# Attention scores from split fp32r operands, a pipeline one step deeper, and one buffer of shifted halves

## The chip, the cores and the metric

The program runs on one core of a Trainium2 chip. The metric is the device time of that core in microseconds, lower is better. Engines are named as the profile names them: PE is TensorE (PEld its weight loads), DVE is VectorE, ACT is ScalarE, POOL is GpSimd, SP issues most DMAs.

## The reference, cut to what matters

A first stage mixes three attentions (compressed, selected, windowed) into `x` of shape (2, 2048, 256), followed by layer norms. The change leaves it alone. Then come two layers of this form, everything in float32:

```python
h = shift_token(x)                     # second half of the channels comes from the token before
q, k, v = split(h @ wqkv)              # 8 heads of 64, 512 columns each
q = l2norm(q) * qs;  k = l2norm(k) * ksc
q, k = rotary_xpos(q, k)
sim = einsum('bhwid,bhwjd->bhwij', bq * 8, look_around(bk))    # 128 queries, 256 keys
o = softmax(where(mask, -big, sim)) @ look_around(bv)
x = x + o @ wo
h = layernorm(shift_token(x)) @ w1 + b1
a, g = split(h)
x = x + (a * gelu(g)) @ w2 + b2
```

The 4096 tokens are 32 blocks of 128. A block of queries sees its own keys and those of the block before.

## The kernel before, in words

One layer is an attention phase over 32 blocks (64 in the two layers) and a feed-forward phase over 8 groups of four blocks. The phases are separated by `end_phase`, at which all engines meet.

**Attention phase.** Each engine has its own function `step(n, i)`, a list of calls in an order fixed by hand. In step n an engine works on several blocks at once, each at another stage: `live(n, lag)` guards a call for block n − lag. The first steps are written out, the middle is a loop of two steps, and the last are written out again. Semaphore waits stand in the called helpers; those under `if type(b) is int` are only in the written-out steps. The calls for one block:

- POOL `stage_h` copies the block and its shifted half (`hs_attn`) to `h_in`. PE `transposes` turns it (L1662). ACT `hi` rounds it to fp32r (`hT_hi`), DVE `lo` subtracts to get the low part `hT_lo` (L2304).
- PE `project(b, 0|1|2)` makes q, k, v in banks 0, 1, 2 as three fp32r products (L1698 to L1700): high by high, high by low, low by high.
- ACT `square` (L1102), DVE `sums` (L2351) with a floor of 1e-24 (L2355), and POOL `root` with the power −1/2 (L771) give the inverse norms. DVE `sines` (L2333) and `cosines` (L2318) multiply the raw q or k by the rotary tables, POOL `add_up` (L785) adds them, DVE `normalise_k` (L2363) scales k.
- PE `turn_qk` transposes q and k (L1722), ACT `q_out` and `k_out` copy them to `qT` and `kT`, which are plain float32.
- PE `scores(b, part)` makes the scores of four heads a part (L1770). A head has 64 channels, so two heads at a time lie in the two halves of the array's rows, and their results go to banks 3 and 4:

```python
for j in (2 * part, 2 * part + 1):
    for e in range(2):
        rows64 = slice(e * DH, (e + 1) * DH)
        mm = pe.matmul(bank[:, 3 + e, ...], qT[rows64, j], kT[rows64, j]..., start=True, stop=True)
```

- DVE `hide` masks a head and takes its maximum (L2436), ACT `exponent` takes the exponential and its sum (L1180), DVE `inverses` inverts two sums and waits for the result (L2465). `weigh` scales a head's probabilities: five heads on DVE (L2471), two on ACT (L1189), one on POOL (L791).
- PE `turn_probs` transposes two heads (L1824), ACT `probs_out` copies them out (L1211), PE `values` multiplies by v (L1856), ACT `values_out` copies that to `oT`, PE `project_out` multiplies by `wo` into bank 5 (L1783), DVE `add_rows` adds to `x_sb` (L2476). `turn_probs(b, 1)` writes bank 5 too, so it waits for `add_rows`. ACT `v_out` copies v to `v_sb` (L1136), into the half that `values` of the block before last has just read, and `project(b, 2)` of the next block waits for it.

**Feed-forward phase.** PE `up` (L1921 to L1923) and `down` (L1936 to L1938) multiply by w1 and w2 as three fp32r products each; `down` has 128 x 256 results. While group g is worked on, the normalised input of the next group is made: DVE `norm_stats`, ACT `norm_apply` (L1283), PE `turn_norm` (L1904), ACT `norm_hi` (L1272), DVE `norm_full` (L2544), POOL `norm_lo` (L826). The last group of a layer does this too, for group 0 again, and nobody uses it. In the second layer ACT also makes the final norm of the group before (`last_norm`, L1293).

**Shifted halves.** SP moves the second half of every block down by one token, to `hs_attn` for the attention phase and to `hs_ffn` for the feed-forward phase.

Of the kernel before, what the change touches and what calls it, by code (L numbers as in the profile page):

```python
# [7 lines left out]
ALU = mybir.AluOpType  # L8
# [5 lines left out]
P = 128  # L14
# [20 lines left out]
MADE = 24  # L35
# [30 lines left out]
def build(nc, x0, Wq, bq, Wk, bk, Wv, bv, Wo, bo, Wg, bg, Wc, bc, Ws, bs,  # L66
          wqkv, q_scale, k_scale, wo, ln_g, ln_b, w1, b1, w2, b2, rope_base, out):
    with ExitStack() as ctx:
# [15 lines left out]
        hs_attn = place("hs_attn", [P, NB + B, P])  # L84
        hs_ffn = place("hs_ffn", [P, NB + B, P])
# [36 lines left out]
        qT = place("qT", [P, HEADS // 2, P])  # L122
        kT = place("kT", [P, HEADS // 2, 2, P])
# [109 lines left out]
        assert base[0] <= hs_at + 8 * (NB + B) * P  # L233
# [9 lines left out]
        HIDDEN = (0, 1, 2, 3, 6, 7, 4, 5)  # L243
        EXPED = (0, 1, 2, 3, 6, 4, 7, 5)
        INVERTED = (0, 1, 3, 2)
        TURNED = (0, 1, 3, 2)
        P_OUT = (0, 1, 3, 2)
        VALUED = (1, 0, 3, 2)
        P_DVE = (1, 0, 2, 4, 6)
        P_ACT = (7, 5)  # L250
        P_POOL = (3,)
# [12 lines left out]

        def later(b, n):

            return min(b + n, NB - 1) if type(b) is int else b + n

        def sin_operand(lay):

            return pT[:] if lay else hs_ffn[:, 1:9, :].rearrange("p (a s) n -> p a (s n)", a=2)
# [116 lines left out]
        qT_ready = sem("qT_ready")  # L388
        v_ready = sem("v_ready")
# [13 lines left out]
        hs_ffn_moved = sem("hs_ffn_moved")  # L403
# [18 lines left out]
        hs_attn_moved = sem("hs_attn_moved")  # L422
# [33 lines left out]
        def _(sp):  # L456
# [68 lines left out]
            def move_group(g):  # L525

                sp.wait_ge(x_made, GB * (g + 1))
                shift_down(hs_attn, g * GB + g // GPB, x_sb[:, g * GB:(g + 1) * GB, P:D], GB, hs_moved)
# [18 lines left out]
            for lay in range(DEPTH):  # L547
# [16 lines left out]
                for first, last in ((0, GB), (GB, NB)):  # L564
                    with sp.Fori(first, last) as t:

                        sp.wait_ge(x_attn, 1 + lay * NB + t + 1)
                        shift_down(hs_ffn, t + t // BPB, x_sb[:, bass.ds(t, 1), P:D], 1, hs_ffn_moved)
                    if first == 0:
                        sp.wait_ge(hs_ffn_moved, 48 * (NB * lay + GB))  # L570
                        settle(sp)
                sp.wait_ge(hs_ffn_moved, 48 * NB * (lay + 1))
# [6 lines left out]
                if lay + 1 < DEPTH:  # L579
# [33 lines left out]
        def _(pool):  # L613
# [54 lines left out]
            pool.wait_ge(sc_made, MADE - 2)  # L668
# [4 lines left out]
            pool.memset(hs_attn[:], 0.0).then_inc(sc_made, 1)  # L673
            pool.memset(hs_ffn[:], 0.0).then_inc(sc_made, 1)
# [57 lines left out]
            for lay in range(DEPTH):  # L732
# [19 lines left out]
                def stage_h(b):  # L752

                    if type(b) is int:
                        if follows(b, 1):
                            pool.wait_ge(hT_ps, k0 + b)
                    settle(pool)
                    pool.tensor_copy(h_in[:, 0], x_sb[:, b, 0:P]).then_inc(h_staged, 1)
                    pool.tensor_copy(h_in[:, 1], hs_attn[:, b + b // BPB, :]).then_inc(h_staged, 1)

                def root(b, which, part):

                    if which == 1:
                        pool.wait_ge(ss_floor[1], k0 + b + 1)
# [3 lines left out]
                    elif which == 0:  # L768
                        pool.wait_ge(ss_floor[0], k0 + b + 1)
# [17 lines left out]
                def weigh(b, h):  # L787

                    pool.wait_ge(inverted, nth(INVERTED, k0 + b, 1))
# [9 lines left out]
                def step(n, i):  # L799
                    if i == 0 and live(n, 4) and live(n, 2):  # L800
# [5 lines left out]
                    if live(n, 0):  # L806
                        stage_h(n)
                    if live(n, 1):
                        add_up(n - 1, 0)
                        root(n - 1, 1, 2)  # L810
                        add_up(n - 1, 1)
# [16 lines left out]
                n0 = lay * (NG + 1)  # L828
# [32 lines left out]
                def group(u, i, first, before):  # L861
# [7 lines left out]
                    norm_scales(n0 + g + 1)  # L869
                    if before:  # L870
                        last_root(g - 1, 1 - i)
                    norm_lo(n0 + g + 1, 1 - i)
# [6 lines left out]
                with pool.Fori(0, NG // 2 - 1) as u:  # L879
                    for i in range(2):  # L880
                        group(u + 1, i, False, last)
                if not last:
# [1813 lines left out]
```

## Time and profile before

| | |
|---|---|
| median of 3 runs | 1615.21 us (1614.42 to 1616.76) |
| the profiled execution, its own time | 1614.17 us |
| its span, first to last instruction | 1612.4 us |
| first stage, up to the first attention phase | 270.5 us |
| attention phase, layer 0 and layer 1 (first L1662 to first L1904) | 445 us and 444 us |
| granted TensorE clock, mean | 0.971 |

Times in the rows are microseconds from the first instruction, unless marked ns. A matmul's time in a row runs to the end of its result, so matmuls that follow each other overlap in the records; the distance between starts is what each one costs PE. A float32 matmul stands as two MATMUL records of half the work, an fp32r matmul and a transpose as one.

### The profile page before, as it was taken

How to read it: one execution, taken by the hardware profiler on the slowest of the kernel's cores; microseconds unless marked ns; L12 is line 12 of the kernel's file. 1: busy time of each engine (PE TensorE's matmuls, PEld its weight loads, DVE VectorE, ACT ScalarE, POOL GpSimd, SP SyncE). 2: the span in 40 equal slices, each digit the busy share in tenths (PEclk: the TensorE clock that was granted, in tenths of full speed). 3: DMA queues.
4: the chain of work that ended last, by engine and by line, in shares of the span. 5: the costliest groups of instructions: out<-in, count | busy, mean ns of one | idle time of the engine just before them, and what ended most of it. 6: DMA issues, size and time to landing. Idle time of an engine off the chain costs nothing.

```text
span 1612.4 us, 34824 instructions
## 1 busy us (share of the span) xinstructions
PE 1505.1 (93%) x9859; PEld 1204.0 (75%) x9859; DVE 1165.4 (72%) x3485; ACT 1009.4 (63%) x2564; POOL 704.5 (44%) x782
## 2 busy tenths in 40 slices
PE   8899992999999999979999959999999999799996
PEld 6467871688787888858888837878787887688885
DVE  6762785888888888875656568888888888666664
ACT  5123574677777777755454538777777778345553
POOL 4013255555555555532222255555555554244442
PEclk9999996999999999999999979999999999899998
DMA  5003134000000000002000020000000000000101
GB/s 174 1 1 110 50 113 126 4 6 6 5 5 5 5 5 5 5 8 87 8 14 7 13 63 5 6 5 5 5 5 5 5 5 7 30 27 27 52 26 52
DMA packets 57513, 43.92 MB, mean 27 GB/s; under 512 B 13214, under 2 KB 55386, under 8 KB 57442
## 3 DMA queue, kind: packets, MB, share of 16 engines
q1 hardware_dynamic: 57442, 43.07, 8.8%
q8 instruction: 33, 0.54, 0.1%
q14 instruction: 38, 0.31, 0.1%
HBM read 26.24 MB, written 8.39 MB: 21 GB/s over the span
## 4 chain that ended last, share of the span: by engine, by line
PE 77%; DVE 9%; ACT 5%; issue 4%; POOL 2%; DVEq 1%; ACTq 1%; DMA 0%; POOLq 0%; SPq 0%; PEldq 0%
PE bank L1770 8%; PE bank L1856 8%; PE bank L1783 7%; PE bank L1824 7%; PE bank L1698 6%; PE bank L1699 5%; PE bank L1700 5%; PE bank L1722 4%; PE bank L1921 3%; PE bank L1922 3%; PE bank L1923 3%; PE bank L1582 2%; PE bank L1936 2%; PE bank L1938 2%; PE bank L1937 2%
## 5 line engine op out<-in xcount | busy, mean ns | idle before, releaser
L771 POOL TENSOR_TENSOR rnorm<-sumsq,neg_half 128x8 f32<-128x8 f32 x128 | 211.0, 1649 | 204.2 <-DVE sumsq L2355 204.2
L1180 ACT ACTIVATE prob<-prob,neg_max 128x256 f32<-128x256 f32 x512 | 253.4, 500 | 1.5 <-DVE neg_max L2436 1.5
L785 POOL TENSOR_TENSOR qk_cos<-qk_cos,qk_sin 128x512 f32<-128x512 f32 x128 | 163.6, 1278 | 132.7 <-DVE qk_cos L2318 131.9
L1698 PE MATMUL bank<-wqkv_hi,hT_hi 128*128 128x512 f32 x384 | 176.9, 461 | 2.9 <-DVE hT_lo L2304 1.9
L1700 PE MATMUL bank<-wqkv_hi,hT_lo 128*128 128x512 f32 x384 | 154.0, 401 | 0.0
L1699 PE MATMUL bank<-wqkv_lo,hT_hi 128*128 128x512 f32 x384 | 153.9, 401 | 0.0
L1921 PE MATMUL bank<-h_hi,w_hi 128*128 128x512 f32 (+1 forms) x352 | 143.2, 407 | 10.3 <-POOL h_lo L826 10.3
L1312 ACT ACTIVATE act_hi<-act_full 128x512 fp32r<-128x512 f32 x96 | 60.9, 634 | 140.5 <-DVE act_full L2622 140.5
L1770 PE MATMUL bank<-kT,qT 64*128 64x256 f32 x1024 | 146.1, 404 | 2.0 <-DVE neg_max L2436 2.0
L1211 ACT ACTIVATE pT<-bank 128x512 f32<-128x512 f32 x256 | 144.5, 591 | 1.9 <-PE bank L1856 1.8
L1923 PE MATMUL bank<-h_lo,w_hi 128*128 128x512 f32 (+1 forms) x352 | 140.9, 400 | 0.0
L1922 PE MATMUL bank<-h_hi,w_lo 128*128 128x512 f32 (+1 forms) x352 | 140.9, 400 | 0.0
L1856 PE MATMUL bank<-pT,v_sb 128*64 128x128 f32 x2048 | 140.2, 279 | 0.5 <-ACT pT L1211 0.5
L2627 DVE TENSOR_TENSOR act_lo<-act_full,act_hi 128x512 fp32r<-128x512 f32 x96 | 87.6, 913 | 69.2 <-ACT act_hi L1312 69.2
L2471 DVE TENSOR_SCALAR prob<-prob,pinv 128x256 f32<-128x256 f32 x320 | 116.0, 396 | 28.8 <-DVE pinv L2465 3.9
L1824 PE MATMUL bank<-ident,prob 128*128 128x128 f32 x1024 | 133.6, 273 | 2.8 <-ACT prob L1189 2.6
L1856 PEld LDWEIGHTS bank<-pT,v_sb 128*64 128x64 f32 x2048 | 109.1, 136 | 32.3 <-ACT pT L1211 21.5
L2622 DVE SCALAR_TENSOR_TENSOR act_full<-bank,b_sb,gelu_sb 128x512 f32<-128x512 f32 x96 | 71.9, 749 | 84.3 <-ACT gelu_sb L1308 60.1
L1783 PE MATMUL bank<-wo_sb,oT 128*128 128x256 f32 x512 | 124.0, 386 | 8.1 <-issue 8.1
L1824 PEld LDWEIGHTS bank<-ident,prob 128*128 128x128 f32 x1024 | 117.4, 141 | 13.3 <-DVE prob L2471 4.1
L1770 PEld LDWEIGHTS bank<-kT,qT 64*128 64x128 f32 x1024 | 88.8, 187 | 42.5 <-issue 33.1
L2333 DVE TENSOR_TENSOR qk_sin<-bank,rope 128x512 f32<-128x512 f32 x128 | 88.6, 692 | 40.8 <-ACT qk_sq L1102 40.8
(270 smaller groups left out, 3721.2 us busy)
## 6 DMA issues: line engine op xcount, KB each, us to landing
x_sb<-in_L_attn_hidden_states SPq DMA_DIRECT2D x8, 512.0 KB, 7.1
x_in<-in_L_attn_hidden_states SPq DMA_DIRECT2D x8, 512.0 KB, 4.5
x_scratch<-x_in SPq DMA_DIRECT2D x8, 512.0 KB, 3.0
f_x<-x_scratch SPq DMA_DIRECT2D x8, 512.0 KB, 4.1
out<-f_y SPq DMA_DIRECT2D x8, 512.0 KB, 3.0
raw<-in_L_ffn_w SPq DMA_DIRECT2D x6, 640.0 KB
hs_attn<-x_sb SPq DMA_DIRECT2D x16, 224.0 KB
hs_ffn<-x_sb SPq DMA_DIRECT2D x64, 56.0 KB, 2.0
```

The costliest lines, as they stand in the source:

```text
L771: pool.tensor_tensor(rnorm[:, part * HEADS:(part + 1) * HEADS], sumsq[:, which * HEADS:(which + 1) * HEADS], neg_half[:, 0:HEADS], ALU.pow ...
L1180: act.activation(prob[:, h], prob[:, h], ACT.Exp, bias=neg_max[:, h:h + 1], scale=-1.0, accum_out=psums[:, h:h + 1]).then_inc(exped, 1)
L1698: pe.matmul(bank[:, to], hT_hi[:, c], wqkv_hi[:, c, cols], start=(c == 0), stop=False)
L1699: pe.matmul(bank[:, to], hT_hi[:, c], wqkv_lo[:, c, cols], start=False, stop=False)
L1700: mm = pe.matmul(bank[:, to], hT_lo[:, c], wqkv_hi[:, c, cols], start=False, stop=(c == DC - 1))
L1770: mm = pe.matmul(bank[:, 3 + e, (j % 2) * 2 * P:(j % 2 + 1) * 2 * P], qT[rows64, j], kT[rows64, j].rearrange("p a b -> p (a b)"), start=Tr ...
L1783: mm = pe.matmul(bank[:, 5, 0:D], oT[:, c], wo_sb[:, c], start=(c == 0), stop=(c == INNER // P - 1))
L1824: tr = pe.transpose(bank[:, 6 - j % 2, ((h % 2) * 2 + c) * P:((h % 2) * 2 + c + 1) * P], prob[:, h, c], ident[:])
L1856: mm = pe.matmul(bank[e * DH:(e + 1) * DH, 7, j * P:(j + 1) * P], v_sb[:, c, h * DH:(h + 1) * DH], pT[:, j % 2, (e * 2 + c) * P:(e * 2 + c ...
L1921: pe.matmul(to, w1_hi[:, c, cols], h_hi[:, half, c], start=(c == 0), stop=False)
L1922: pe.matmul(to, w1_lo[:, c, cols], h_hi[:, half, c], start=False, stop=False)
L1923: mm = pe.matmul(to, w1_hi[:, c, cols], h_lo[:, half, c], start=False, stop=(c == DC - 1))
```

## The change

Four things change.

- `qT` and `kT` become fp32r, `qT_lo` and `kT_lo` are new. DVE makes them (`q_lo`, `k_lo`) by subtracting the rounded values from banks 0 and 1. `scores` makes three products, q by k, q by k_lo, q_lo by k.
- Of DVE's five heads, head 1 is now scaled by ACT and head 4 by POOL; the floor of 1e-24 moves from DVE to POOL (`root`).
- Every engine's step is put in another order with another set of lags; the output projection is five blocks behind instead of four. Eight steps ahead of the loop and five behind it are written out, instead of six and four.
- `hs_attn` and `hs_ffn` become one buffer `hs`. The last group of a feed-forward phase no longer makes a next input, and the last two groups are written out behind the loop. POOL clears one buffer less, ACT clears `kT_lo` once a layer more.

```diff
-        qT = place("qT", [P, HEADS // 2, P])
-        kT = place("kT", [P, HEADS // 2, 2, P])
+        qT = place("qT", [P, HEADS // 2, P], F32R)
+        kT = place("kT", [P, HEADS // 2, 2, P], F32R)
-        P_DVE = (1, 0, 2, 4, 6)
-        P_ACT = (7, 5)
-        P_POOL = (3,)
+        P_DVE = (0, 2, 6)
+        P_ACT = (1, 7, 5)
+        P_POOL = (3, 4)
...
                     for j in (2 * part, 2 * part + 1):
-                        for e in range(2):
-                            rows64 = slice(e * DH, (e + 1) * DH)
-                            mm = pe.matmul(bank[:, 3 + e, (j % 2) * 2 * P:(j % 2 + 1) * 2 * P], qT[rows64, j],
-                                           kT[rows64, j].rearrange("p a b -> p (a b)"), start=True, stop=True)
+                        for n, (q, k) in enumerate(((qT, kT), (qT, kT_lo), (qT_lo, kT))):
+                            for e in range(2):
+                                rows64 = slice(e * DH, (e + 1) * DH)
+                                mm = pe.matmul(bank[:, 3 + e, (j % 2) * 2 * P:(j % 2 + 1) * 2 * P], q[rows64, j],
+                                               k[rows64, j].rearrange("p a b -> p (a b)"), start=(n == 0), stop=(n == 2))
...
+                def q_lo(b):
+                    dve.wait_ge(qT_ready, k0 + b + 1)
...
+                    dve.tensor_tensor(qT_lo[:], bank[:, 0].rearrange("p (c t) -> p c t", t=P), qT[:], ALU.subtract).then_inc(qT_lo_ready, 1)
+                def k_lo(b, half):
+                    dve.wait_ge(kT_ready, k0 + b + 1)
...
+                    dve.tensor_tensor(kT_lo[:, :, half], bank[:, 1].rearrange("p (c t) -> p c t", t=P), kT[:, :, half], ALU.subtract).then_inc(kT_lo_ready, 1)
...
-                    dve.tensor_scalar(sumsq[:, part], sumsq[:, part], 1e-24, None, ALU.max).then_inc(ss_floor[which], 1)
+                    pool.tensor_scalar(some, some, 1e-24, None, ALU.max).then_inc(ss_floor[which], 1)
+                    pool.wait_ge(ss_floor[which], k0 + b + 1)
...
-                        if j == 3:
+                        if j == 3 and more(u * 2 + i):
                             turn_norm(n + 1)
```

The order of a step on PE, in the loop, before: `project_out` (n − 4), v of n − 1, the input transposes of n, k turned, the probabilities of n − 2, then q of n:

```order
L1783 MATMUL bank<-wo_sb,oT 128x256 x4
L1698 MATMUL bank<-wqkv_hi,hT_hi 128x512
...
L1662 MATMUL bank<-ident,h_in 128x128 x2
L1722 MATMUL bank<-ident,qk_cos 128x128 x4
L1824 MATMUL bank<-ident,prob 128x128 x4
...
L1770 MATMUL bank<-kT,qT 128x256 x4
```

and after the change (the products are L1730 to L1732, scores L1811, probabilities turned L1865, values L1897, q and k turned L1758):

```order
L1824 MATMUL bank<-wo_sb,oT 128x256 x4
L1730 MATMUL bank<-wqkv_hi,hT_hi 128x512
...
L1865 MATMUL bank<-ident,prob 128x128 x4
...
L1811 MATMUL bank<-kT,qT 128x256 x2
L1811 MATMUL bank<-kT_lo,qT 128x256 x2
L1811 MATMUL bank<-kT,qT_lo 128x256 x2
...
L1897 MATMUL bank<-pT,v_sb 64x128 x4
L1758 MATMUL bank<-ident,qk_cos 128x128 x4
```

Four float32 matmuls of a part became twelve fp32r ones (the three rows shown stand twice in a part); k of n − 1 is now projected first, both parts stand behind a projection or the values, and k and q are turned together near the end of the step.

On DVE, around `add_rows` (writes `x_sb`) and `lo` (writes `hT_lo`) in the loop, the order before is

```order
L2363 TENSOR_TENSOR qk_cos<-qk_cos,rnorm 128x512
...
L2465 RECIPROCAL pinv<-psums 128x2
...
L2471 TENSOR_SCALAR prob<-prob,pinv 128x256 x2
...
L2476 TENSOR_TENSOR x_sb<-bank,x_sb 128x256
...
L2304 TENSOR_TENSOR hT_lo<-bank,hT_hi 128x256
L2351 TENSOR_REDUCE sumsq<-qk_sq 128x8
L2355 TENSOR_SCALAR sumsq<-sumsq 128x8
```

and after the change, over the end of a step and the beginning of the next,

```order
L2413 TENSOR_TENSOR kT_lo<-bank,kT 128x4x128
...
L2527 RECIPROCAL pinv<-psums 128x2
...
L2345 TENSOR_TENSOR hT_lo<-bank,hT_hi 128x256
L2533 TENSOR_SCALAR prob<-prob,pinv 128x256 x2
...
L2527 RECIPROCAL pinv<-psums 128x2
...
L2403 TENSOR_TENSOR qT_lo<-bank,qT 128x512
...
L2538 TENSOR_TENSOR x_sb<-bank,x_sb 128x256
```

Before, `add_rows` (there L2476) stood ahead of `hT_lo` (L2304) of the same step, and nothing of the kind of `kT_lo` and `qT_lo` existed; now `add_rows` comes behind `hT_lo`, two scaled heads, a reciprocal and `qT_lo` of the step before.

## Rows read from the trace of the kernel before

**Rows 1.** The page's busy times of the engines over the whole span.

```profile
PE 1505.1 (93%) x9859; PEld 1204.0 (75%) x9859; DVE 1165.4 (72%) x3485; ACT 1009.4 (63%) x2564; POOL 704.5 (44%) x782
```

**Rows 2.** Busy times in one step of the attention loop; the first row names the columns.

```profile
core 0: us, PE busy (x) PEld busy (x) DVE busy (x) ACT busy (x) POOL busy (x), PEclk, DMA share, GB/s
410.72:424.00 13.28, 13.28 (x101) 10.64 (x101) 10.80 (x37) 10.38 (x30) 7.07 (x9) 1.00 0.02 5
```

**Rows 3.** The chain that ended last, same step: start, us, what.

```profile
410.72 1.73 PE bank L1783 x8
412.68 0.23 PE bank L1699
...
419.43 0.87 PE bank L1824 x8
420.30 1.02 PE bank L1856 x16
421.32 1.06 PE bank L1770 x8
...
424.00 1.73 PE bank L1783 x8
```

**Rows 4.** Timeline of one score part: start, us, engine, line; two, then eight matmuls.

```profile
403.42 0.49 PE L1770 MATMUL bank<-kT,qT 64*128 64x256 f32 x2
403.42 0.73 PEld L1770 LDWEIGHTS bank<-kT,qT 64*128 64x128 f32 x8 [0.36 <-issue]
403.42 1.13 PE L1770 MATMUL bank<-kT,qT 64*128 64x256 f32 x8
```

**Rows 5.** Timeline of PE in the feed-forward phase, ends of twelve matmuls of `down`.

```profile
819.31 0.28 PE L1936 MATMUL bank<-w_hi,act_hi 128*128 128x256 f32 x1
...
820.73 0.39 PE L1921 MATMUL bank<-h_hi,w_hi 128*106 128x512 f32 x1
```

**Rows 6.** Groups of DVE, 400 to 500 us: busy us, mean ns, idle before.

```profile
L2471 DVE TENSOR_SCALAR prob<-prob,pinv 128x256 f32<-128x256 f32 x38 | 13.9, 399 | 3.3 <-DVE pinv L2465 0.2
L2333 DVE TENSOR_TENSOR qk_sin<-bank,rope 128x512 f32<-128x512 f32 x15 | 10.4, 692 | 4.2 <-ACT qk_sq L1102 4.2
...
L2465 DVE RECIPROCAL pinv<-psums 128x2 f32<-128x2 f32 x30 | 4.8, 161 | 1.7 <-DVE pinv L2465 1.7
L2304 DVE TENSOR_TENSOR hT_lo<-bank,hT_hi 128x256 fp32r<-128x256 f32 x8 | 3.4, 425 | 6.5 <-ACT hT_hi L1089 6.5
L2476 DVE TENSOR_TENSOR x_sb<-bank,x_sb 128x256 f32 x8 | 3.2, 405 | 0.0
L2355 DVE TENSOR_SCALAR sumsq<-sumsq 128x8 f32<-128x8 f32 x15 | 2.6, 172 | 2.6 <-DVE sumsq L2351 0.8
```

**Rows 7.** Groups of ACT and POOL in the same stretch.

```profile
L1136 ACT ACTIVATE v_sb<-bank 128x512 f32<-128x512 f32 x7 | 4.2, 598 | 3.3 <-PE bank L1856 3.3
...
L771 POOL TENSOR_TENSOR rnorm<-sumsq,neg_half 128x8 f32<-128x8 f32 x15 | 24.7, 1648 | 25.9 <-DVE sumsq L2355 25.9
...
L791 POOL TENSOR_SCALAR prob<-prob,pinv 128x256 f32<-128x256 f32 x8 | 5.1, 640 | 7.5 <-DVE pinv L2465 7.5
```

**Rows 8.** The chain through the first steps of layer 0.

```profile
270.53 0.68 PE bank L1662 x2
...
277.63 0.61 ACT qk_sq L1102
...
283.13 0.66 PE bank L1722 x4
...
285.83 2.03 PE bank L1770 x8
```

**Rows 9.** Feed-forward phases: layer 0 and end of layer 1, two chain rows, one timeline row.

```profile
814.39 0.87 PE bank L1904 x8
...
1592.71 1.57 ACT f_y L1293 x3
...
1597.50 0.38 PE L1936 MATMUL bank<-w_hi,act_hi 42*128 42x256 f32 x1 [2.17 <-DVE act_lo L2627]
```

More of the change, by code:

```diff
@@ L83, in build @@
         hs_at = base[0]
[L84 to L85 removed]
+        hs = place("hs", [P, NB + B, P])
+        qT_lo = place("qT_lo", [P, HEADS // 2, P], F32R)
+        kT_lo = place("kT_lo", [P, HEADS // 2, 2, P], F32R)
+        sin_0 = place("sin_0", [P, 2, BPB * 32])
+        place("spare", [P, 10 * P])
         ident = place("ident", [P, P])
@@ L263, in follows, with more @@
             return type(b) is not int or b >= n
+        def more(g):
+            return type(g) is not int or g + 1 < NG
         def later(b, n):
@@ L878, in _ @@
                 group(0, 1, False, last)
-                with pool.Fori(0, NG // 2 - 1) as u:
+                with pool.Fori(0, NG // 2 - 2) as u:
                     for i in range(2):
                         group(u + 1, i, False, last)
+                for i in range(2):
+                    group(NG // 2 - 1, i, False, last)
                 if not last:
@@ L1072, in _ @@
                 act.wait_ge(x1_stored, 16 * NG)
-                act.activation(kT[:, :, 1], zero[:, 0:1, None].broadcast_to([P, HEADS // 2, P]), ACT.Copy).then_inc(kv_zero, 1)
+                for k in (kT, kT_lo):
+                    act.activation(k[:, :, 1], zero[:, 0:1, None].broadcast_to([P, HEADS // 2, P]), ACT.Copy).then_inc(kv_zero, 1)
                 act.activation(v_sb[:, 1], zero[:].broadcast_to([P, INNER]), ACT.Copy).then_inc(kv_zero, 1)
@@ L1264, in _ @@
                         step(u * 2 + i, i)
-                for n in range(NB, NB + 3):
+                for n in range(NB, NB + 4):
                     step(n, n % 2)
@@ L1327, in _ @@
                 group(0, 1, False, last)
-                with act.Fori(0, NG // 2 - 1) as u:
+                with act.Fori(0, NG // 2 - 2) as u:
                     for i in range(2):
                         group(u + 1, i, False, last)
+                for i in range(2):
+                    group(NG // 2 - 1, i, False, last)
                 if not last:
@@ L1962, in _ @@
                     group(0, i, i == 0)
-                with pe.Fori(0, NG // 2 - 1) as u:
+                with pe.Fori(0, NG // 2 - 2) as u:
                     for i in range(2):
                         group(u + 1, i, False)
+                for i in range(2):
+                    group(NG // 2 - 1, i, False)
                 for j in range(FC - 2, FC):
@@ L2636, in group @@
                             last_moments(g - 1, 1 - i)
-                        if j == 3:
+                        if j == 3 and more(g):
                             norm_full(n)
@@ L2647, in _ @@
                 group(0, 1, False, last)
-                with dve.Fori(0, NG // 2 - 1) as u:
+                with dve.Fori(0, NG // 2 - 2) as u:
                     for i in range(2):
                         group(u + 1, i, False, last)
+                for i in range(2):
+                    group(NG // 2 - 1, i, False, last)
                 add_up(lay * NG + NG - 1, NG - 1)
```

411 lines of the change are left out of this document (223 added, 188 removed).

## The prediction

> **What bounds the kernel now.** I read the busy times first: PE is busy in 93% of the span, the next engine, DVE, in 72% [rows 1]. An average hides stages, so I then cut one step out of the attention loop [rows 2]: PE is busy in all of its 13.28 us at the full granted clock, while DVE has 10.80 us of work, ACT 10.38 and POOL 7.07. The chain of waits says the same in another way [rows 3]: from one output projection (410.72) to the next (424.00) every piece is a piece of PE, and it waits for nobody. The loop therefore costs what PE's matmuls cost. DVE has 2.5 us of room in a step, ACT 2.9, POOL 6.2. The 64 blocks at 13.28 us would be 850 us of the 1614, so a change of 0.1 us a step moves the total by 6.4 us.
>
> What PE pays for: a 512-column fp32r matmul 0.23 us, eight transposes 0.87, sixteen value matmuls 1.02, the output projection 1.73, and a score part 1.06, twice a step [rows 3].
>
> **The score parts, the term that carries the sum.** A part before is four float32 matmuls, eight records. The first two together end after 0.49 us, all eight after 1.13 [rows 4], so the three later pairs follow at (1.13 − 0.49) / 3 = 0.213 us. The two heads of a pair thus run at once, in the two halves of the rows: eight in a row at 0.213 would be 1.70 us, and the part takes 1.06. Of these 1.06, 4 x 0.213 = 0.85 is streaming, and 0.21 is the first weight load and the switch into and out of half arrays.
>
> A part now is six pairs of fp32r matmuls of 256 columns. No row shows an fp32r pair in half arrays. The nearest row is `down`, fp32r with 256 columns over the full array: twelve of them take 820.73 − 819.31 = 1.42 us, 0.118 each, and every one has its own weights, so their loads are hidden [rows 5]. I take 0.118 for a pair, since the float32 pair shows that a second head costs nothing [rows 4]. The part becomes 0.21 + 6 x 0.118 = 0.92 us, 0.14 less. The number of switches between full and half arrays in a step stays six. Over 128 parts: **−17.9 us**. Bounds: half of the float32 pair's 0.213 is 0.107, which would save another 0.07 a part, 8 us in all; no overlap of the two heads is the other end, a rival below.
>
> One rule speaks against taking 0.118. The rows of the float32 part show that loads run under matmuls of the same half: eight loads end 0.73 us after the start, the matmuls 1.13 [rows 4]. The Trainium skill (TensorE: Matmul & The Clock Gate, Part 3 on packing small matmuls) says that a weight load overlaps matmuls in flight only if its row group differs, though Part 2 of the page also allows it for a load into the background buffer. By the sentence of Part 3 the total would be the second rival's, 1666 us; the trace sides with Part 2.
>
> **DVE.** New: `qT_lo` and `kT_lo`, each 128 x 512 from PSUM. Of that form is the sine product, 692 ns [rows 6]; twice is +1.38 us a step. Gone: two floors, 2 x 0.172, and two of five scaled heads, 2 x 0.399. DVE goes from 10.80 to about 11.04 us, plus some 0.2 us behind each reciprocal, in a step of 13.0. It is covered by PE with nearly 2 us left, so the work itself costs nothing; if PE's cover went, all of 0.24 us a step would show.
>
> **ACT and POOL.** ACT gets one head, 0.5 us: 10.9 in 13.0. POOL gets one head, 0.64 [rows 7], and two floors, each under the 0.64 of that much larger operation and perhaps 0.3: 7.07 becomes 8.3. Costs nothing. A floor now stands ahead of the power of 1.65 us [rows 7] and lengthens the way to `rnorm` by about 0.2 us, but its readers, the masks, come a step later.
>
> **The order.** What decides is whether a wait ends late. I laid the step out, PE from the start of `project_out`: k 1.73 to 3.13, four heads turned to 4.0, scores to 5.0, q to 6.5, turned to 7.4, values to 8.4, scores to 9.4, values to 10.5, k and q turned to 11.4, v to 12.8, input transposes to 13.0. Then I put the others behind it. The tight places:
> - `turn_probs(1)` waits for `add_rows`. After the input transposes DVE has `hT_hi` by ACT (about 0.4 and 0.2 to get there), `hT_lo` 0.43, two heads 0.80, a reciprocal with its wait 0.38, `qT_lo` 0.69, `add_rows` 0.41 [rows 6]: 3.3 us. PE meanwhile has 1.73 + 6 x 0.23 + 0.44 = 3.57 [rows 3]. Slack 0.25.
> - `project` of v waits for `v_out`, which waits for the last values: 0.60 [rows 7] and 0.3 of handing over, against eight transposes and a switch, about 1.0. Slack 0.1 to 0.2.
> - The second score part waits for four masks: 2.4 us after the first part, against 3.3 us of PE work. Slack 0.9. k turned waits for POOL's sum and `normalise_k`: slack 0.6 or more. Input transposes wait for the last mask: 0.7.
>
> All are positive, so the loop stays PE's, at 13.28 − 0.28 = **13.00 us**. SP's moves come one step later and are not waited for in the loop. Since two slacks are small, I charge 0.02 us a step, +1.2 us.
>
> **Filling and draining.** Before, the first score part begins 15.3 us after the first transposes and itself takes 2.03 us, twice its time in the loop; v of block 0 lies under the way from the squares (277.63) to the turned k (283.13) [rows 8]. Now v stands behind the turned k and q, so that way is bare, and `qT_lo` is added: I make it 16.9 us. The second part waits 0.8 us longer for masks, and k of block 2 waits for `hT_lo`; against that come the cheaper parts, already counted. About +2.4 us. At the drain one more step stands, but the same work lies behind the last scores: 0 to −0.5. Bounds +0.5 and +5 a layer; I take 2, for two layers **+4 us**.
>
> **The feed-forward phases.** Turning the unused input goes: 0.87 us of PE [rows 9] in each layer. At the very end PE stands 2.17 us before the last `down`: ACT's final norm (from 1592.71) and the unused norms before it delay the last activation [rows 9]. ACT and DVE lose more than PE there; I give the second layer 1.6. Together **−2.5 us**. The two groups written out are the same instructions: 0. The merged buffer: slot t is overwritten five steps after it was read, no wait: 0. POOL's cleared buffer lies in a wait, ACT's extra one beside POOL's rotary tables: 0.
>
> **Sum.** −17.9 + 1.2 + 4 − 2.5 = −15.2 us. Against the profiled execution's own 1614.17 this is 1599; its median counterpart is 1615.21, 1.0 above, so **1600.0 us**. A measurement of this kernel can tell about 0.2% from no change, 3.2 us.
>
> **Rivals.**
> 1. *Small waits eat the gain.* If `v_out` or `add_rows` is late by 0.1 to 0.24 us a step, 64 steps give back 6 to 15 us: 1606 to 1615. For: slacks of 0.1 to 0.25 are as small as my errors of handing over. Against: DVE and ACT have 2 us of room. 13%.
> 2. *Loads are bare.* If each pair first waits for its weights, by half of the 0.21 beside the streaming, a pair costs 0.118 + 0.105: the part becomes 6 x 0.223 + 0.105 = 1.44, 0.38 more than now, 128 of them +49, total 1666. The trace of float32 speaks against it [rows 4]. 4%.
> 3. *The two heads of an fp32r pair run one after the other* (the other side, slower). Place: PE's score parts. Twelve times 0.118 plus 0.21 is 1.63, +0.57 a part, +73 us, total 1691. It decides from a pair of 0.136 us up: from there the parts give back the whole 15 us. For: fp32r streams a column in 0.46 ns, faster than a float32 record, and no row shows two such streams. Against: two heads of 64 rows read no more than one full array does [rows 5]. 5%.
> 4. *The DVE chain becomes a bound*, above 0.24 us late a step: slower than before, 1618 to 1635. 4%.
> 5. *Better than forecast*: pairs at 0.107, or filling free: 1586 to 1594. 7%.
>
> **Numbers.** The forecast, 1595 to 1606, has 67%. The range 1591 to 1616 adds nearly all of rival 1 and half of 5, about 83%. Faster: 67 + 7 + 8 of rival 1's 13, 0.82. Within 0.2%: the other 5, 0.05. Slower: 4 + 5 + 4, 0.13.
>
> **What would show it.** In the changed trace a score part should last 0.92 us on the chain, with 12 records, and six pairs 0.12 apart; the output projections should lie 13.00 us apart, and PE should have no idle time but in the first three steps of a layer. DVE should be busy 11.0 to 11.3 us a step. PE waits on `x_sb` or `v_sb` in the loop would be rival 1; starts of a pair 0.12 apart instead of 0.01 rival 3; 0.22 between pairs rival 2. A step above 13.28 makes the forecast wrong, and so does a fill above 20 us.

## The result, and the profile after

| | before | after |
|---|---|---|
| median | 1614.42 us (1613.72 to 1616.76, 5 runs) | 1606.59 us (1605.55 to 1607.81, 5 runs) |
| span of the profiled execution | 1612.4 us | 1604.8 us |

The ratio is 0.9948, interval 0.9934 to 0.9963: faster by 0.5%, 8 us. The forecast was 15 us. The busy times of the page, against [rows 1]:

```profile
PE 1488.4 (93%) x10355; PEld 1218.0 (76%) x10355; DVE 1175.1 (73%) x3329; ACT 1025.1 (64%) x2610; POOL 771.9 (48%) x961
```

Two steps of the loop, cut from one output projection to the next, against [rows 2], with the same columns:

```profile
413.95:427.05 13.10, 13.10 (x111) 10.95 (x110) 11.11 (x35) 10.71 (x31) 8.45 (x11) 1.00 0.02 5
427.05:440.06 13.01, 13.01 (x111) 10.79 (x109) 11.22 (x35) 10.79 (x31) 8.26 (x10) 1.00 0.02 5
```

PE is still busy in all of both, at the full granted clock. A step is 13.10 and 13.00 us in turn, 13.05 on average, where it was 13.28. Where that comes from stands in PE's timeline of one score part, between the turned probabilities and the projection of q (start, us, engine, line, what), against [rows 4]:

```profile
418.12 0.39 PE L1811 MATMUL bank<-kT,qT 64*128 64x256 f32 x2
418.34 0.28 PE L1811 MATMUL bank<-kT_lo,qT 64*128 64x256 f32 x2
418.46 0.28 PE L1811 MATMUL bank<-kT,qT_lo 64*128 64x256 f32 x2
418.57 0.28 PE L1811 MATMUL bank<-kT,qT 64*128 64x256 f32 x2
418.69 0.29 PE L1811 MATMUL bank<-kT_lo,qT 64*128 64x256 f32 x2
418.81 0.29 PE L1811 MATMUL bank<-kT,qT_lo 64*128 64x256 f32 x2
419.03 0.50 PE L1730 MATMUL bank<-wqkv_hi,hT_hi 128*128 128x512 f32 x1
```

Six pairs: the second to the sixth start 0.11 to 0.12 us apart, the first and the last take 0.22 each, with the switch into and out of half arrays. That makes 419.03 − 418.12 = 0.91 us for the part. It was 1.06.

So the loop gains nearly what was forecast, and more than half of that is gone elsewhere. I cut both traces at the same places: the first input transposes of a layer, the second score part of block 2, that of block 31, the first turned norm. The fill is the stretch of first steps in which the pipeline is not yet full, the drain the one of last steps.

| us | before, layers 0 and 1 | after | forecast a layer |
|---|---|---|---|
| up to the first attention phase | 270.5 | 270.0 | 0 |
| to the second part of block 2 (the fill) | 44.5, 42.9 | 48.5, 49.1: **+4.0, +6.3** | +2, less 0.7 for five cheaper parts |
| from there to block 31, 29 steps | 382.4, 382.3 | 376.0, 376.0: **−6.4, −6.3** | −7.5 |
| from there to the turned norm | 18.3, 19.3 | 18.9, 18.9 | −0.1 to −0.6 |
| feed-forward phase | 223.3, 228.9 | 220.9, 226.6: **−2.4, −2.4** | −0.9, −1.6 |

The fill is the surprise. PE's timeline there, layer 0, first of the kernel before and then of the changed one; the bracket is PE's idle time and who ended it:

```profile
278.53 0.66 PE L1722 MATMUL bank<-ident,qk_cos 128*128 128x128 f32 x4 [0.94 <-POOL qk_cos L785]
278.95 0.48 PE L1698 MATMUL bank<-wqkv_hi,hT_hi 128*128 128x512 f32 x1
...
280.43 0.38 PE L1662 MATMUL bank<-ident,h_in 128*128 128x128 f32 x2
283.13 0.66 PE L1722 MATMUL bank<-ident,qk_cos 128*128 128x128 f32 x4 [2.32 <-DVE qk_cos L2363]
```

```profile
276.34 0.40 PE L1732 MATMUL bank<-wqkv_hi,hT_lo 128*128 128x512 f32 x1
281.17 1.97 PE L1758 MATMUL bank<-ident,qk_cos 128*128 128x128 f32 x8 [4.43 <-DVE qk_cos L2421]
282.79 0.78 PE L1730 MATMUL bank<-wqkv_hi,hT_hi 128*128 128x512 f32 x1
...
285.50 0.63 PE L1690 MATMUL bank<-ident,h_in 128*128 128x128 f32 x2
287.06 0.50 PE L1730 MATMUL bank<-wqkv_hi,hT_hi 128*128 128x512 f32 x1 [0.93 <-DVE hT_lo L2345]
...
292.95 0.39 PE L1811 MATMUL bank<-kT,qT 64*128 64x256 f32 x2 [1.72 <-DVE neg_max L2494]
294.75 0.66 PE L1758 MATMUL bank<-ident,qk_cos 128*128 128x128 f32 x4 [0.82 <-DVE qk_cos L2421]
295.88 0.66 PE L1758 MATMUL bank<-ident,qk_cos 128*128 128x128 f32 x4 [0.46 <-POOL qk_cos L798]
...
299.08 0.50 PE L1730 MATMUL bank<-wqkv_hi,hT_hi 128*128 128x512 f32 x1 [0.93 <-DVE hT_lo L2345]
...
311.55 0.50 PE L1730 MATMUL bank<-wqkv_hi,hT_hi 128*128 128x512 f32 x1 [0.93 <-DVE hT_lo L2345]
```

Before, q is turned at once, and the 1.5 us of v and the input transposes of block 1 (278.95 to 280.8) lie under the wait for the turned k. After the change the way from the squares through POOL's power to the turned k is bare: 4.43 us. Behind it the same work comes late and at half clock: v's six matmuls start 0.43 us apart instead of 0.23 (282.79 to 285.50, 2.7 us with the first load, for 1.5), and then the next block's `hT_lo` is bare too.

The waits add up as follows. At the first turned q and k PE idles 4.43 us, where it idled 0.94 + 2.32 before: 1.2 more. The masks ahead of the second score part cost 1.72 for 1.00, the turned k and q of block 1 0.82 + 0.46 for none. And PE waits 0.93 us for `hT_lo` three times more, 2.8 us, the largest piece; waits of 0.41 and 0.54 us for `v_sb` and a mask are gone. That is some 5 us more idle time, of which the cheaper score parts leave the 4.0 of the table. No wait here is ended by SP's moves or by POOL's fourth head. The floor on POOL adds 0.12 us to a way: from the end of the sums to the start of the power it is 0.62 us (275.83 to 276.45) and was 0.50 (278.95 to 279.45).

Busy times and granted clock of the same three stretches of layer 1, before and after:

```profile
939.05:954.20 15.15, 10.96 (x42) 7.74 (x44) 5.55 (x11) 3.64 (x7) 5.89 (x6) 0.76 0.56 148
954.20:969.20 15.00, 12.90 (x77) 8.78 (x74) 13.53 (x46) 10.10 (x31) 8.56 (x11) 1.00 0.00 1
969.20:982.00 12.80, 12.69 (x110) 9.84 (x107) 11.31 (x38) 11.25 (x33) 7.83 (x9) 1.00 0.01 3
```

```profile
934.86:950.00 15.14, 9.73 (x29) 7.31 (x28) 6.62 (x9) 3.08 (x6) 5.06 (x7) 0.66 0.58 148
950.00:965.00 15.00, 10.48 (x57) 7.80 (x58) 10.67 (x33) 7.75 (x24) 8.36 (x13) 0.89 0.01 2
965.00:984.00 19.00, 18.07 (x163) 14.68 (x163) 16.63 (x50) 15.56 (x42) 13.76 (x17) 1.00 0.01 1
```

PE is idle 42.95 − 36.55 = 6.4 us before and 49.14 − 38.28 = 10.9 after: 4.5 of the 6.2 us (42.95 to 49.14) are idle time. In the other 1.7 PE does the same work as before but for the score parts, which are cheaper, so what is left is the lower clock (0.66 and 0.89 granted, for 0.76 and 1.00).

### The profile page after: what moved, and what is told of

The parts are those of the page before. It is cut to its first block, busy times and chain, and to the rows that moved or that the text cites. A ratio compares the mean times of both kernels' runs of the same rounds, so it can differ in the third digit from the quotient of the medians.

```text
span 1604.8 us, 35975 instructions
## 1 busy us (share of the span) xinstructions
PE 1488.4 (93%) x10355; PEld 1218.0 (76%) x10355; DVE 1175.1 (73%) x3329; ACT 1025.1 (64%) x2610; POOL 771.9 (48%) x961
## 4 chain that ended last, share of the span: by engine, by line
PE 80%; DVE 8%; ACT 4%; issue 3%; POOL 2%; DVEq 1%; DMA 0%; ACTq 0%; POOLq 0%; SPq 0%; PEldq 0%
PE bank L1897 8%; PE bank L1811 7%; PE bank L1865 7%; PE bank L1824 7%; PE bank L1730 6%; PE bank L1732 6%; PE bank L1731 6%; PE bank L1758 4%; PE bank L1960 4%; PE bank L1961 4%; PE bank L1962 4%; PE bank L1975 2%; PE bank L1610 2%; PE bank L1977 2%; PE bank L1976 2%
## 5 line engine op out<-in xcount | busy, mean ns | idle before, releaser
L798 POOL TENSOR_TENSOR qk_cos<-qk_cos,qk_sin 128x512 f32<-128x512 f32 x128 | 180.5, 1411 | 50.9 <-DVE qk_cos L2359 48.9
L1730 PE MATMUL bank<-wqkv_hi,hT_hi 128*128 128x512 f32 x384 | 178.5, 465 | 7.5 <-DVE hT_lo L2345 7.5
L1126 ACT ACTIVATE qk_sq<-bank 128x512 f32<-128x512 f32 x128 | 76.9, 601 | 133.8 <-PE bank L1732 133.8
L1732 PE MATMUL bank<-wqkv_hi,hT_lo 128*128 128x512 f32 x384 | 154.6, 403 | 0.0
L1897 PE MATMUL bank<-pT,v_sb 128*64 128x128 f32 x2048 | 140.2, 279 | 0.5 <-ACT pT L1237 0.5
L1237 ACT ACTIVATE pT<-bank 128x512 f32<-128x512 f32 x256 | 137.9, 592 | 1.7 <-PE bank L1897 1.7
L1865 PE MATMUL bank<-ident,prob 128*128 128x128 f32 x1024 | 133.4, 273 | 3.5 <-DVE prob L2533 2.4
L1865 PEld LDWEIGHTS bank<-ident,prob 128*128 128x128 f32 x1024 | 118.9, 141 | 22.8 <-DVE prob L2533 3.5
L2494 DVE CUSTOM_DVE_ANT_0 prob<-bank,mask_odd,rnorm 128x256 f32<-128x256 f32 x256 | 115.4, 480 | 24.1 <-PE bank L1811 13.2
L2494 DVE CUSTOM_DVE_ANT_0 prob<-bank,mask_even,rnorm 128x256 f32<-128x256 f32 x256 | 115.7, 480 | 18.5 <-DVE pinv L2527 7.2
L1897 PEld LDWEIGHTS bank<-pT,v_sb 128*64 128x64 f32 x2048 | 109.1, 136 | 20.4 <-issue 10.3
L2392 DVE TENSOR_REDUCE sumsq<-qk_sq 128x8 f32<-128x512 f32 x128 | 87.4, 683 | 36.5 <-ACT qk_sq L1126 36.2
```

The lines of the kernel that those rows point to most:

```text
L1730: pe.matmul(bank[:, to], hT_hi[:, c], wqkv_hi[:, c, cols], start=(c == 0), stop=False)
L1732: mm = pe.matmul(bank[:, to], hT_lo[:, c], wqkv_hi[:, c, cols], start=False, stop=(c == DC - 1))
L1865: tr = pe.transpose(bank[:, 6 - j % 2, ((h % 2) * 2 + c) * P:((h % 2) * 2 + c + 1) * P], prob[:, h, c], ident[:])
L1897: mm = pe.matmul(bank[e * DH:(e + 1) * DH, 7, j * P:(j + 1) * P], v_sb[:, c, h * DH:(h + 1) * DH], pT[:, j % 2, (e * 2 + c) * P:(e * 2 + c ...
L2494: dve.tensor_tensor_reduce(prob[:, h].rearrange("p a b -> p (a b)"), bank[:, 3 + h % 2, (h // 2 % 2) * 2 * P:(h // 2 % 2 + 1) * 2 * P], ma ...
```

## The experiments

My theory after this result: the products save 19 us or so, the unused norm 2.5 to 4, and the new order gives back about 10 in the fill and adds nothing in the loop. The rival: the new order and the lighter DVE are what makes room for the low parts, and the fill is the price. A smaller question was why every second step takes 0.1 us more. All ratios are against the kernel before, run beside it.

### The products back to float32

```diff
-        qT = place("qT", [P, HEADS // 2, P], F32R)
-        kT = place("kT", [P, HEADS // 2, 2, P], F32R)
+        qT = place("qT", [P, HEADS // 2, P])
+        kT = place("kT", [P, HEADS // 2, 2, P])
...
-                        for n, (q, k) in enumerate(((qT, kT), (qT, kT_lo), (qT_lo, kT))):
+                        for n, (q, k) in enumerate(((qT, kT),)):
```

> The changed kernel with the old products: qT and kT are float32 again and a part is four float32 matmuls; DVE still makes qT_lo and kT_lo, which nobody reads. Theory A (the split products carry the gain): a part goes from 0.91 back to 1.06 us, a step from 13.05 to 13.35, 128 parts give 19 us, total about 1625, slower than the kernel before by 10, since the fill of the new order stays. Rival B (the new order and the lighter DVE carry the gain, the products only part of it): under 1615.

Measured: 1625.33 us, ratio 1.0072 (1.0058 to 1.0086). Steps of 13.40 and 13.29, PE busy in all of one:

```profile
418.00:431.40 13.40, 13.40 (x102) 10.81 (x101) 11.08 (x35) 10.70 (x30) 8.51 (x11) 1.00 0.02 5
```

The products alone are worth 1.0072 − 0.9948, 1.2% or 20 us, more than the whole change brings. All the rest together costs 11 us: in this run's trace the fills are 9.7 us longer than before and the two times 29 steps 4.9, against 3.6 less in the feed-forward phases. So with the same float32 products a step of the new order is not free either: 13.40 and 13.29 us in turn for 13.28.

### The kernel before without the unused norm

```diff
-                        if j == 3:
+                        if j == 3 and more(u * 2 + i):
                             turn_norm(n + 1)
```

and the same guard at the other engines' calls, with the last two groups written out.

> The kernel before with only the last group's unused norm left out and the last two groups written out. In the trace of the changed kernel the two feed-forward phases are 2.4 and 2.35 us shorter, where 0.87 and 1.6 were forecast. Theory A: all of that is this part, total 4.7 us less, 1609.7. Rival B: it is the 0.87 of PE and the last activations alone, 2.5 us less, 1612, and the rest comes from elsewhere (the merged buffer).

Measured: 1610.90 us, ratio 0.9979 (0.9970 to 0.9988), −3.4 us, between the two theories. From the first matmul of `up` to the last of `down` a layer takes 1.1 and 2.0 us less than before; in the changed kernel it takes 1.5 and 2.5 less, and what the 0.5 a layer come from stays open. The other 0.9 that the feed-forward phase of the changed kernel gains in layer 0 is the way from the first turned norm to the first `up`, which takes 6.2 to 7.1 us in different executions: scatter.

### An earlier start in the fill of the changed kernel

```diff
+                    if type(n) is int and n == 1:
+                        project(n - 1, 2, v_raw)
+                        transposes(n)
+                        turn_qk(n - 1, 1)
+                        turn_qk(n - 1, 0)
+                        return
```

on PE, with `hi(1)` and `lo(1)` moved ahead on ACT and DVE.

> The changed kernel; in step 1 of a layer alone, v of block 0 and the input transposes of block 1 stand ahead of the turned k and q on PE, and hT of block 1 is made earlier by ACT and DVE. Theory A (the new order lays bare the way from the squares to the turned k, PE idles 4.4 us and its clock halves for the next 6.8): PE idles 2 us or less there, the first score part begins about 15 us after the first transposes instead of 18.7, 3.5 to 4 us less a layer, total 1599. Rival B (the fill is bound by the chain through DVE and POOL in step 2, root of q behind stage_h): 1 us less a layer or nothing, 1605 to 1607.

Measured: 1602.75 us, ratio 0.9932 (0.9918 to 0.9945), about 2.6 us less than the changed kernel by the ratios, 3.2 in the two fills of the traces. The first score part comes 16.4 and 16.9 us after the first transposes instead of 18.7 and 17.9, but of these 2.3 and 1.1 us layer 0 keeps only 0.7 to the second part of block 2, while layer 1 gains 2.4. The result lies between the two theories. The place was right, the size not: v now lies in the wait, but what is left of it still stands, another wait appears behind the turned q, and the clock is half again just behind them.

```profile
280.88 1.09 PE L1760 MATMUL bank<-ident,qk_cos 128*128 128x128 f32 x8 [2.96 <-DVE qk_cos L2429]
283.20 0.76 PE L1732 MATMUL bank<-wqkv_hi,hT_hi 128*128 128x512 f32 x1 [1.24 <-DVE kT_lo L2421]
```

### PE's loop of four steps

```diff
-                with pe.Fori(4, NB // 2) as u:
-                    for i in range(2):
-                        step(u * 2 + i, i)
+                with pe.Fori(2, NB // 4) as u:
+                    for i in range(4):
+                        step(u * 4 + i, i % 2)
```

> The changed kernel with four steps instead of two in PE's loop. In its trace steps last 12.99 and 13.10 us by turns, and the longer one has 0.10 more in the output projection, the first work behind the loop's jump. Theory A (the jump bares the first weight load): three steps of four last 12.99, half of 24 jumps a layer less at 0.10, 1.2 to 2.5 us less, total 1604.5 to 1605.5. Rival B (another wait of even and odd steps, as POOL's mask copy): steps still alternate, no change.

Measured: 1604.40 us, ratio 0.9945 (0.9932 to 0.9959). Steps of 12.99, 12.99, 13.09, 12.99: the 0.1 us belongs to the jump of PE's loop, since the other engines' loops were left as they are. Right behind it stands `project_out`, whose 1.54 us become 1.64. It is worth 0.7 us a layer in the trace, too little for the medians.

### The old order with the split products

```diff
+                        pe.wait_ge(lo_ready, 2 * (k0 + b) + 2)
...
                     if live(n, 1):
+                        q_lo(n - 1)
                         normalise_k(n - 1)
...
                         sums(n - 1, 0)
+                        k_lo(n - 1, 1 - i)
```

`lo_ready` counts both low parts; the products are those of the change; the buffers of the low parts lie where `w2_lo` does, which is written only later.

> The kernel before, in its old order, with the three fp32r products and the two subtractions alone (q_lo ahead of normalise_k, k_lo behind the sums of q's squares; all five heads stay on DVE). Theory A, the order and the lighter DVE are needed to harvest the cheap products: by the rows of before, qT_lo fits, but kT_lo can end at 416.6 where the scores begin at 416.70, everything behind it on DVE is 0.6 us later, and the second score part then finds its fourth mask about 0.2 to 0.3 us late; DVE has 12.2 us of work a step. Steps of 13.1 to 13.35 us, total 1606 to 1616 with a DVE-released PE wait ahead of the second part, and a shorter fill than the changed kernel's (q still a step ahead). Theory B, the order is not needed: steps of 12.98 us, total 1595 to 1600, better than the changed kernel, because its fill stays that of before plus about 1 us.

Measured: 1608.68 us, ratio 0.9966 (0.9953 to 0.9979). Steps of 12.98 and 13.35 in layer 0, 12.98 and 13.15 in layer 1: the total is in theory A's range, the average step (13.17 and 13.07 us) at the lower end of its steps, and the wait is at another place than it had. It is not the fourth mask but `add_rows`, in `turn_probs(1)`:

```profile
426.12 0.41 DVE L2507 TENSOR_TENSOR x_sb<-bank,x_sb 128x256 f32 x1
```

```profile
426.75 0.65 PE L1835 MATMUL bank<-ident,prob 128*128 128x128 f32 x4 [0.19 <-DVE x_sb L2507]
```

and DVE is idle for 0.3 us in the 5.7 ahead of that row, both times behind a reciprocal. The fill is much nearer to that of before, 44.9 and 44.8 us for 44.5 and 42.9.

### The changed kernel with one product

```diff
-                        for n, (q, k) in enumerate(((qT, kT), (qT, kT_lo), (qT_lo, kT))):
+                        for n, (q, k) in enumerate(((qT, kT),)):
```

> The changed kernel with only the first of the three products (q by k in fp32r); the two low parts are still made, nobody reads them, so the scores are less exact. Theory A, PE is the bound and nothing stands close behind: four pairs of 0.116 us go from each part, a part becomes 0.45 us, a step 13.05 - 0.93 = 12.12 us, total 1606 - 60 = 1547 us. Theory B, the chain of DVE and ACT is close behind PE (11.1 us of work on DVE and some 0.2 us behind each reciprocal): steps of 12.3 to 12.7 us with PE waiting for x_sb, v_sb or masks, total 1558 to 1585 us.

Measured: 1583.82 us, ratio 0.9815 (0.9801 to 0.9829); steps of 12.55 and 12.72, not 12.12. Of the 0.93 us taken from a step only 0.41 come through. The next bound is close behind PE, as theory B said, but it is at the turned q and not at `x_sb`, `v_sb` or a mask:

```profile
417.13 0.60 ACT L1126 ACTIVATE qk_sq<-bank 128x512 f32<-128x512 f32 x1 [1.51 <-PE bank L1732]
...
421.18 0.68 DVE L2374 TENSOR_TENSOR qk_sin<-bank,rope 128x512 f32<-128x512 f32 x1
...
421.78 0.68 DVE L2359 TENSOR_TENSOR qk_cos<-bank,rope 128x512 f32<-128x512 f32 x1
...
422.64 1.56 POOL L798 TENSOR_TENSOR qk_cos<-qk_cos,qk_sin 128x512 f32<-128x512 f32 x1 [0.66 <-DVE qk_cos L2359]
...
424.44 0.63 PE L1758 MATMUL bank<-ident,qk_cos 128*128 128x128 f32 x4 [0.50 <-POOL qk_cos L798]
```

That way goes from the projected k over ACT's squares to DVE, through the sums, products and masks that DVE has in its order ahead of q's two products, and over POOL's addition. POOL's power (419.07 to 420.74) is not on it. Its slack in the changed kernel is thus about 0.4 us, and not the 0.25 at `add_rows` that I had as the smallest.

### Heads 1 and 4 back on DVE

```diff
-        P_DVE = (0, 2, 6)
-        P_ACT = (1, 7, 5)
-        P_POOL = (3, 4)
+        P_DVE = (0, 1, 2, 6, 4)
+        P_ACT = (7, 5)
+        P_POOL = (3,)
```

> The changed kernel with heads 1 and 4 scaled on DVE again, as before. DVE gets 0.8 us more a step, 11.9 in 13.05. Theory A, the slack that I forecast for add_rows ahead of the second turning of probabilities (0.25 us) is right: head 1 stands in that chain with 0.4 us, PE waits 0.15 us a step for x_sb, total 1614 to 1617 us. Theory B, the slack is 0.4 us or more and the rebalancing is worth nothing in this order: steps of 13.05 us, total 1605 to 1608 us.

Measured: 1610.06 us, ratio 0.9977 (0.9968 to 0.9986). Neither theory's number: 3.5 us more than the changed kernel by the medians, 4.7 by the ratios. In the trace the step grows in layer 0 alone, to 13.18 in the steps with the jump (1.8 us over the layer), and again at the turned k and q, 1.00 us instead of 0.87:

```profile
425.24 1.24 PE L1755 MATMUL bank<-ident,qk_cos 128*128 128x128 f32 x8
426.24 0.48 PE L1727 MATMUL bank<-wqkv_hi,hT_hi 128*128 128x512 f32 x1
```

No wait for `x_sb` appears, so that slack was 0.4 us or more. The remaining 1.7 to 2.9 us I can't place in the trace; they stay open.

### POOL's sum of q behind the scaled k

```diff
                     elif which == 0:
...
+                            if b == 0:
+                                pool.wait_ge(qk_ready[1], k0 + 1)
```

> The changed kernel with one wait more: POOL's sum of q of block 0 waits for DVE's normalise_k of block 0, in each layer's fill. Theory A, the 1.73 us of that normalise_k (0.68 in the loop) come from DVE and POOL working on SBUF at the same time: it takes 0.70 us, k is turned 1.0 us earlier, q about 0.5 later than k, the first score part begins 18.1 us after the first transposes instead of 18.7; total 1 us less, 1605 to 1606. Theory B, the 1.73 has another cause (the first use, the low clock of the fill): it stays 1.7, POOL's sum begins only behind it, the fill becomes 0.8 to 1.0 us longer a layer, total 1608.

Measured: 1606.90 us, ratio 0.9956 (0.9942 to 0.9970). In the changed kernel, DVE's `normalise_k` of block 0 and POOL's two additions:

```profile
279.38 1.73 DVE L2421 TENSOR_TENSOR qk_cos<-qk_cos,rnorm 128x512 f32<-128x512 f32 x1 [0.69 <-POOL qk_cos L798]
```

```profile
278.09 2.48 POOL L798 TENSOR_TENSOR qk_cos<-qk_cos,qk_sin 128x512 f32<-128x512 f32 x2
```

and with the added wait:

```profile
279.85 0.69 DVE L2423 TENSOR_TENSOR qk_cos<-qk_cos,rnorm 128x512 f32<-128x512 f32 x1 [0.54 <-POOL qk_cos L800]
```

```profile
280.81 1.26 POOL L800 TENSOR_TENSOR qk_cos<-qk_cos,qk_sin 128x512 f32<-128x512 f32 x1 [1.00 <-DVE qk_cos L2423]
```

The cause is theory A's: the two operations were in each other's way. The gain is not: the first score part comes 19.6 and 18.0 us after the first transposes, no earlier. PE's timeline with the added wait, layer 0:

```profile
282.13 1.12 PE L1760 MATMUL bank<-ident,qk_cos 128*128 128x128 f32 x4 [0.42 <-POOL qk_cos L800]
...
287.16 0.79 PE L1732 MATMUL bank<-wqkv_hi,hT_hi 128*128 128x512 f32 x1 [0.93 <-DVE hT_lo L2347]
...
290.02 0.58 PE L1813 MATMUL bank<-kT,qT 64*128 64x256 f32 x2
```

Counted from the first transposes (269.96 in the changed kernel, 270.42 here), k is turned 1.0 us earlier, q 0.4 and v begins 0.35 earlier. Behind that the clock takes it back: the six matmuls from the wait for `hT_lo` to the first score part last 290.02 − 287.16 = 2.86 us at half clock, where the changed kernel has them at full clock in 288.66 − 287.06 = 1.60. In layer 1 v and the input transposes behind it run at half clock for longer, and the 0.35 us are gone by `hT_lo`. So a shorter wait in the fill was worth only what the granted clock left of it.

### Both fills and the loop together

```diff
-                    if live(n, 1):
+                    if type(n) is int and n == 2:
+                        project(n - 1, 2, v_raw)
+                        turn_qk(n - 1, 1)
+                        turn_qk(n - 1, 0)
+                    elif live(n, 1):
```

on top of the early start and the loop of four, with `v_out(0)` a step earlier on ACT.

> The changed kernel with three edits together: the early start of e3_fill (v of block 0 and the input transposes of block 1 ahead of the first turned k), the same for v of block 1 one step later, and PE's loop of four steps instead of two. Theory A, the fill and the jump are what the changed kernel leaves on the table, and they add up: 1602.8 of e3_fill, minus 2 times 0.7 for the jumps, minus 2 times 0.5 for v under the second wait for the turned k: 1600 to 1601 us. Theory B, the fill's waits only move to the next late thing: 1602 to 1604 us.

Measured: 1602.69 us, ratio 0.9923 (0.9909 to 0.9937). The trace shows the attention phases at 440.5 and 439.2 us, 2.2 less each than with the early start alone, more than theory A's 1.2; the medians show nothing over it (1602.75). By the medians it is theory B's range, and the difference is inside the scatter: inconclusive.

### The old order with one head less on DVE

```diff
-        P_DVE = (1, 0, 2, 4, 6)
-        P_ACT = (7, 5)
+        P_DVE = (0, 2, 4, 6)
+        P_ACT = (1, 7, 5)
...
                         exponent(n - 1, 3)
+                        weigh(n - 1, 1)
```

on top of the old order with the split products and of the left-out unused norm.

> The order of the kernel before, with the fp32r products and subtractions of e5_before_split, head 1 scaled by ACT instead of DVE, and the last group's unused norm left out. In e5_before_split PE waited in every second step, 0.41 us in layer 0 and 0.20 in layer 1, for x_sb, with DVE never idle there. Theory A, DVE was only overfull: with one head off DVE (0.4 us a step) every step is 12.98 us, 30 times 0.18 and 30 times 0.08 us go, and with 3 us of the unused norm the total is 1597 to 1599 us; the new order is not needed, and it costs its longer fill. Theory B, the old order cannot hold the two low parts ahead of its scores whatever DVE's load (kT_lo ends 0.3 us behind the scores' turn): a wait of 0.2 us or more a step stays, now ahead of the scores, total 1604 to 1610 us.

Measured: **1596.60 us** (1594.81 to 1598.83), ratio 0.9882 (0.9867 to 0.9898): 18 us faster than before and 10 faster than the changed kernel. A step, with every engine's busy time:

```profile
409.50:422.50 13.00, 13.00 (x111) 10.82 (x110) 11.76 (x38) 10.71 (x31) 7.26 (x9) 1.00 0.02 5
```

The steps are 12.97 to 13.03 us, though DVE has 11.8 us of work. Against the old order with all heads on DVE, the 29 steps are 4.4 and 1.7 us shorter, the fills 0.3 and 1.7, and the unused norm is 3.4: 11.5 of the 12.1 us between the two medians. The fill of layer 1 is nearly that of before, in the same three stretches:

```profile
932.99:948.10 15.11, 11.82 (x48) 8.58 (x48) 7.31 (x14) 3.75 (x7) 6.08 (x6) 0.74 0.59 148
948.10:963.10 15.00, 12.03 (x82) 8.79 (x80) 13.98 (x45) 10.57 (x31) 8.12 (x11) 1.00 0.01 3
963.10:976.20 13.10, 12.76 (x118) 9.91 (x114) 12.05 (x39) 11.52 (x34) 7.92 (x9) 1.00 0.00 1
```

Against the changed kernel the fill is shorter by 3.9 and 6.0 us (44.6 and 43.2 for 48.5 and 49.1), together 9.9. The medians differ by 10.0, the two profiled executions by only 7.7: the 29 steps of both layers are 1.1 us shorter here, but the first stage, the drains and the feed-forward phases are 3.3 us longer, 1.5 of it in the first stage, whose code is the same. So the new order isn't needed for the split products; in the old order one head moved off DVE is enough, and the new order pays with its fill. This kernel also leaves head 4 and the floor on DVE and keeps two buffers of shifted halves. Their share was not run by itself; in the timeline of the fill the floor is 0.12 us a time, and the other two end no wait.

## Why the prediction was right in sign and half in size

- **The score part** was forecast from `down` at 0.118 us a pair and 0.92 a part: 0.116 to 0.12 and 0.91. The two heads of a pair start together. Rivals 2 and 3 are out. The trace also decides between Part 2 and Part 3 of the Trainium skill's page (TensorE: Matmul & The Clock Gate) that I quoted: the pairs have weights of their own in the same half and still follow at 0.12 us, so loads run under matmuls of the same rows. This term is −19 us, where I had −17.9 (the run with float32 products gives 19 to 20).
- **The loop** is PE's, and no wait for `x_sb` or `v_sb` shows in it. The step is 13.05 and not 13.00: half of the steps carry 0.1 us of the jump. Before, the jump stands behind four transposes of q and doesn't show; now it stands behind two input transposes and does. I charged 0.02 a step for late waits; what came was 0.05, of another kind. Of the slacks, `add_rows` had more than the 0.25 I gave it. I had laid out the turned k alone, with 0.6 or more; the turned q right behind it has 0.4, less than that.
- **DVE, ACT, POOL** were forecast at 11.04, 10.9 and 8.3: 11.1 to 11.2, 10.7 to 10.8 and 8.3 to 8.5.
- **The fill** is the step that failed: "I take 2, for two layers +4 us", with bounds of 0.5 to 5 a layer. Measured it is +4.0 and +6.3, and with the five cheaper parts in it 4.7 and 7.0, some 12 in all. I saw that v would no longer cover the way to the turned k, and put the first score part at 16.9 us; it came at 18.7 and 17.9. What I left out: v and the input transposes of block 1 now stand behind the turned q, and the first scores stand behind block 1's k, so v's time and the bare way to `hT_lo` (0.93) are added to the chain instead of overlapping it; the engine that idled 4.4 us then runs at half clock; and the output projection that in the loop covers `hT_lo` isn't there in the first steps, so it is 0.93 three times in each layer, where I named it once, and the turned k and q of block 1 are waited for too (1.3). The 0.8 us for the masks ahead of the second part came as 0.7. I laid out the first part and estimated the next two steps.
- **The feed-forward phases** were −2.5 and are −3.4 by the run that has this part alone, −4.8 in the trace of the changed kernel, of which 0.9 in layer 0 are scatter.
- **The drain** and the other zeros hold: 0.6 more and 0.4 less, within the scatter.

The time lies in the range that I gave rival 1, but its mechanism, a late `v_out` or `add_rows`, isn't there. That the range held is thus partly luck: it was as wide as it was for another reason. The misses are 8 us in the fill and 2.4 in the loop on the one side, some 3 in the feed-forward phases and the first stage on the other: 7.6 us less gain than forecast.

## What to carry to other kernels

A new order of a software pipeline has two prices, one for a step and one for the fill, and the second is paid once for every phase. Lay out the first three steps as carefully as the steady one: what covered a long chain in the loop, or in the old fill, may stand behind it now. Count a bare wait as often as there are steps without the work that covers it. And try the cheap part of a change in the old order first: here it needed one head moved to another engine, and nothing else.

## What the runs showed of the hardware

- *DVE and POOL block each other on SBUF.* `normalise_k` (both operands in SBUF) takes 0.69 us alone and 1.73 when POOL's addition, also from SBUF, is under way (279.38). The other way round, POOL's addition takes 1.56 instead of 1.26 where it starts 0.27 us behind DVE in the loop (423.15, behind 422.88). DVE's products from PSUM take 0.68 beside the same addition (278.01). The Trainium skill (SBUF — State Buffer, on its two separate sides) has it as an exclusive lock, for a VectorE operation with two SBUF inputs against a GpSimd operation that reads SBUF, whoever starts first: the rows agree, as 1.73 is the rest of POOL's second addition (to 280.57) and DVE's own time less 0.15 us of overlap.
- *The loop's jump* costs PE 0.1 us in one order and nothing in the other, though `project_out` stands behind it in both: 1.64 us for 1.54 behind two input transposes, 1.54 in every step behind four transposes of q.
- *The clock.* Layer 0 of the changed kernel, around the wait of 4.43 us:

```profile
276.00:279.00 3.00, 0.74 (x3) 0.31 (x1) 2.31 (x4) 0.60 (x1) 2.79 (x3) 0.96 1.03 367
279.00:283.00 4.00, 1.83 (x9) 1.83 (x10) 2.38 (x3) 0.60 (x1) 1.57 (x2) 0.58 0.65 196
283.00:287.00 4.00, 3.13 (x9) 2.04 (x8) 1.06 (x3) 0.98 (x2) 0.70 (x3) 0.56 0.00 0
```

The granted clock falls from full, 2.4 GHz, to half, 1.2 GHz, at about 279.7, still in the wait (276.74 to 281.17), and stays there to about 286.5, through the work that comes behind it: six matmuls took 2.7 us instead of 1.5. Before, with waits of 0.94 and 2.32 us there, it was halved later and for less time (284.3 to 287.7, a mean of 0.66 in 283 to 287). A wait in this fill can thus cost more than its length.
